# Causal mask of the key-major scores: added in the banks by VectorE instead of put there by TensorE

## The chip, the core and the metric

The kernel runs on one core of one Trainium2 chip. The metric is the device time of one execution in microseconds. Lower is better. Before the change the median of three runs is 4985.88 us (4983.53 to 4986.44).

## The reference

64 sequences of 256 tokens (x) with 256 channels go through two blocks. Each also has a context of 77 tokens. In short:

```
# block L0: cross attention to the context, 16 heads of 64
q0 = rms(x) @ wq ; k0, v0 = ctx @ wk, ctx @ wv
x  = x + softmax(q0 k0^T) v0 @ wo
# block L1, 16 heads of 16: causal self attention
z1 = ln(x)
q, k, v = z1 @ mq + b, z1 @ mk + b, z1 @ mv + b
scores  = q k^T / 4 ;  scores = where(t >= s, scores, -inf)
x  = x + softmax(scores) v @ m_proj + b
# then cross attention to the context, and the feed-forward layer
x  = x + attention(ln(x), ctx) @ c_proj + b
x  = x + relu(ln(x) @ f_w1 + b1) @ f_w2 + b2
```

All is float32. The kernel keeps that accuracy by splitting operands into a high and a low part and making three products for one.

## The kernel before

**Stages.** The keys and values of the context are made first for all sequences (steps ct, ka, va, up to about 330 us). Then every sequence ("batch" in the code) goes through the same steps, named in USES: turn.0 (transposes of x), q0, qs0.t.g (scores of block L0, queries on partitions), tr0 (transposes of the probabilities), pv0, wo; turn.1, q1.1, k1, v1, qsA and qsB (scores of the self attention, queries on partitions, used only for the maxima and sums of the rows), mt.1 (maxima plus logarithms of the sums, transposed, into maxT), skA.0, skA.1, skB (the same scores once more, but with keys on partitions: key-major), pv.1.0, pv.1.1, proj.1.0, proj.1.1; turn.2, q1.2, qs2, mt.2, sk2, pv.2, proj.2 (the second cross attention); turn.3, h.0 to h.3, f2.0, f2.1 (feed-forward, result to DRAM). rms, stat and norm are the statistics and the normalising, ln makes the logarithms' part of maxT's source. The last number is mostly a tile of 128 tokens or a half of the heads.

**Key-major scores.** skA.m has the first 128 keys against all 256 queries for the eight heads of half m. It fills four banks, one for each row r of the array of 32 partitions, with two heads to a bank. skB has the last 128 keys against the last 128 queries for all 16 heads, four heads to a bank. For each step TensorE makes, bank by bank, three kinds of products (lines 1566 to 1585): the mask on the diagonal blocks of 128 x 128 (line 1572: causal times a unit matrix, both bf16; it also starts the bank), minus the maxima and logarithms (line 1578, from maxT), the scores (line 1583, k1bd with q1T). ScalarE takes the exp of a whole bank of 512 (line 1041) into probs, and pv.1.m multiplies it with v1. The mask of the query-major scores (line 1531) is a product too, and is not touched.

**Order.** The loop is a software pipeline: in one turn TensorE does the steps of three sequences in the order written out in LOOP_ORDER_TEXT; a step with + belongs to the newest sequence, one with - to the oldest, and a step without a sign to the one between (the numbers after the colon are its banks). ScalarE and VectorE have their own written orders, ACT_ORDER_TEXT and DVE_ORDER_TEXT (after a slash: the part, one bank of four, or for qs0 the maximum 0 and the scaling 1). GpSimd and SyncE walk TensorE's order and do what belongs to them: GpSimd the inverse roots (line 904) and the additions of a bias row to xr and x1 (lines 919, 925), SyncE the loads and stores. There are 61 turns; HEAD and TAIL hold the steps ahead of the loop and behind it, with orders of their own. The last turns in the tail hold fewer sequences.

**Waits.** Every bank has two counting semaphores: full (TensorE is done with it) and free (its last reader is). take_bank waits for the bank's former reader, landed for the readers that made a step's operands. All engines run their orders strictly, so an instruction that waits holds up all that stand behind it on its engine. TensorE also passes 230 empty waits ahead of the work, which shift the place of its instructions.

## Time and profile before

| what | us |
|---|---|
| median of three runs | 4985.88 |
| the profiled execution, its own time | 4985.86 |
| its span in the profile | 4984.1 |
| TensorE busy | 4801.7 (96%) |
| ScalarE busy | 3932.9 (79%) |
| VectorE busy | 3063.4 (61%) |
| GpSimd busy | 538.1 (11%) |

The busy time of TensorE is a union of matmuls that overlap in the array, and their ends are modelled. So a step's cost on TensorE is better read from the start of its first matmul to the start of the next step's. A group's "idle before" is the time for which its engine stood still ahead of it, with what ended that. PEld is the loading of weights, which lies beside the matmuls.

### The profile page before, as it was taken

Reading aid. Unit: us, or ns where it says so; the run is one execution under the profiler, and the core shown is the slowest. Engines: PE = TensorE matmul, PEld = TensorE weight load, DVE = VectorE, ACT = ScalarE, POOL = GpSimd, SP = SyncE. Lnnn points to the kernel's source line nnn. Section 1 sums busy time; section 2 is a strip of 40 time slices with the busy share of each in tenths; the row PEclk is TensorE's granted clock in tenths of the full one; section 3 lists DMA queues with packets and bytes.
Section 4 is the critical chain, followed back from the end, with each engine's and each line's share of the span. In section 5 each row is a group of like instructions: output and inputs, shape, how many; then the busy total and the mean of one; then the engine's idle time right before and its main releaser. Section 6 shows DMA issues by size and latency. Waiting matters only on the chain.

```text
span 4984.1 us, 142324 instructions
## 1 busy us (share of the span) xinstructions
PE 4801.7 (96%) x47160; PEld 3896.2 (78%) x47160; DVE 3063.4 (61%) x8003; ACT 3932.9 (79%) x16437; POOL 538.1 (11%) x845
## 2 busy tenths in 40 slices
...
DMA packets 219919, 181.12 MB, mean 36 GB/s; under 512 B 111312, under 2 KB 203920, under 8 KB 219856
## 3 DMA queue, kind: packets, MB, share of 16 engines
...
q8 instruction: 38, 0.62, 0.1%
q14 instruction: 25, 0.20, 0.0%
...
## 4 chain that ended last, share of the span: by engine, by line
issue 61%; PE 26%; POOL 8%; DVE 3%; ACT 1%; POOLq 0%; DMA 0%; DVEq 0%; SPq 0%
PE ps L1398 7%; PE ps L1400 6%; PE ps L1399 6%; POOL xr L919 3%; POOL small L904 3%; PE ps L1594 3%; PE ps L1512 2%; POOL x L925 2%; DVE z L1183 1%; DVE stats L1161 1%; PE ps L1406 1%; DVE x L1298 1%; ACT ps L952 0%; PE ps L1611 0%; DVE mv L1165 0%
## 5 line engine op out<-in xcount | busy, mean ns | idle before, releaser
L952 ACT ACTIVATE ps<-ps,negmax 128x77 f32<-128x77 f32 (+2 forms) x6144 | 2082.7, 380 | 64.9 <-DVE negmax L1197 64.9
L952 ACT ACTIVATION_READ_ACCUMULATOR ps<-ps,negmax 128x1 f32 x6144 | 1526.4, 257 | 0.0
L1197 DVE TENSOR_REDUCE negmax<-ps 128x4 f32<-128x308 f32 (+2 forms) x1792 | 932.1, 561 | 575.6 <-PE ps L1502 380.2
L904 POOL TENSOR_TENSOR small<-small 128x1 f32<-128x1 f32 (+1 forms) x448 | 265.8, 593 | 3974.7 <-DVE small L1174 2137.1
L1041 ACT ACTIVATE probs<-ps 128x512 f32<-128x512 f32 x768 | 396.5, 604 | 321.0 <-PE ps L1583 321.0
L1502 PE MATMUL ps<-k0bd,q0T 128*128 128x154 f32 x2048 | 360.4, 298 | 0.1
L932 ACT COPY probs<-ps 77x512 f32<-77x512 f32 x512 | 286.8, 590 | 62.1 <-PE ps L1545 62.0
L1502 PEld LDWEIGHTS ps<-k0bd,q0T 128*128 128x128 f32 x2048 | 289.8, 191 | 27.0 <-issue 25.9
L1398 PE MATMUL ps<-hi_f,coTh 128*128 128x256 f32 x1024 | 303.4, 296 | 2.5 <-DVE coTl L1332 2.5
L1398 PE MATMUL ps<-zTh,hi_f 128*128 128x256 f32 x1024 | 300.8, 294 | 4.3 <-DVE zTl L1192 3.1
L1398 PE MATMUL ps<-xTh,hi_wq 128*128 128x256 f32 x1024 | 300.7, 294 | 4.3 <-issue 4.3
L1398 PE MATMUL ps<-hi_wo,coTh 128*128 128x256 f32 x1024 | 296.2, 289 | 2.1 <-ACT ps L952 2.1
L1545 PE MATMUL ps<-ident,rows 128*77 128x128 f32 x2048 | 292.1, 280 | 4.7 <-DVE rows L1274 0.4
L1399 PE MATMUL ps<-lo_f,coTh 128*128 128x256 f32 x1024 | 290.1, 283 | 0.0
L1400 PE MATMUL ps<-hi_f,coTl 128*128 128x256 f32 x1024 | 289.4, 283 | 0.0
L1399 PE MATMUL ps<-lo_wo,coTh 128*128 128x256 f32 x1024 | 289.4, 283 | 0.0
L1400 PE MATMUL ps<-hi_wo,coTl 128*128 128x256 f32 x1024 | 289.4, 283 | 0.0
L1400 PE MATMUL ps<-zTh,lo_f 128*128 128x256 f32 x1024 | 289.1, 282 | 0.0
L1399 PE MATMUL ps<-zTl,hi_f 128*128 128x256 f32 x1024 | 289.0, 282 | 0.0
L1399 PE MATMUL ps<-xTl,hi_wq 128*128 128x256 f32 x1024 | 287.7, 281 | 0.0
L1400 PE MATMUL ps<-xTh,lo_wq 128*128 128x256 f32 x1024 | 287.3, 281 | 0.0
L1545 PEld LDWEIGHTS ps<-ident,rows 128*77 128x77 f32 x2048 | 226.0, 147 | 75.9 <-issue 57.4
(226 smaller groups left out, 12477.7 us busy)
## 6 DMA issues: line engine op xcount, KB each, us to landing
keys_of<-kring SPq DMA_DIRECT2D x128, 154.0 KB, 1.9
k0bd<-keys_of SPq DMA_DIRECT2D x128, 154.0 KB, 3.2
...
```

Source lines behind the costliest of these rows:

```text
L904: nc.gpsimd.tensor_tensor(rstd[:, stage, ts], veps[:, stage, ts], minus_half[:, ts], ALU.pow).then_inc(rstd_ready[stage], 1)
L919: nc.gpsimd.tensor_tensor(xr[:, t, :], xs[:, t, :], row[:, k - 1, :], ALU.add).then_inc(xr_ready, 1)
L932: return nc.scalar.copy(o, i)
L952: ins = nc.scalar.activation(scores, scores, ACT.Exp, bias=negmax[w][:, t, h:h + 1], accum_out=sums[w][:, t, h:h + 1])
L1041: nc.scalar.activation(probs_slot(step, r), bank(s), ACT.Exp).then_inc(free[s], 1)
L1197: nc.vector.tensor_reduce(dst, bank(s)[:, 0:heads * width].rearrange("p (h k) -> p h k", h=heads), AX_X, ALU.max, negate=True).then_inc(ma ...
L1398: pe.matmul(o, lh, rh, start=first, stop=False)
L1399: pe.matmul(o, lh, rl, start=False, stop=False)
L1400: return pe.matmul(o, ll, rh, start=False, stop=last)
L1502: ins = pe.matmul(bank(s)[:, j * 2 * S:(j + 1) * 2 * S], q0T[:, m, t * P:(t + 1) * P], k0bd[:, m, :, :], start=True, stop=True)
L1545: ins = pe.transpose(bank(s)[0:S, j * P:(j + 1) * P], rows_of_four(t, g)[:, j * S:(j + 1) * S], ident[:])
L1594: ins = pe.matmul(bank(s)[D0 * e:D0 * e + D0, j * T:(j + 1) * T], v0[0:S, D0 * h:D0 * h + D0], probs_slot(("tr0", 0, i), e)[0:S, j * T:(j ...
```

## The change

The four mask products in front of skA.0, skA.1 and skB go. Their first product with maxT starts the bank now. VectorE gets a step for each bank: it waits for full, adds a mask tile causal_keys (bf16, made by GpSimd at the start) to the diagonal blocks in the bank, in place, and counts a new semaphore, masked, for which ScalarE's exp waits in place of full. An add has 2 x 128 elements in each partition for skA and 4 x 128 for skB. The mask for the query-major scores stays on TensorE. With this all orders, all banks of the steps, and the sequence to which tr0.0.0 and tr0.1.0 belong in a turn are written anew, in the loop, the end of the head and the tail. The tail's orders are now the loop's three times over with the missing steps left out.

```diff
-RINGS = {"bank": 8, "split": 1, "chain": 1, "max": 1, "summed": 1}
+RINGS = {"bank": 8, "split": 1, "chain": 1, "max": 1, "masked": 1, "summed": 1}
...
-    "skA": {"bank": 4}, "skB": {"bank": 4}, "sk2": {"bank": 4},
+    "skA": {"bank": 4, "masked": 4}, "skB": {"bank": 4, "masked": 4}, "sk2": {"bank": 4},
...
 LOOP_ORDER_TEXT = """
-rms+ pv.1.0:1 skA.1:4357 tr0.0.0-:6 qs0.0.2-:0 pv0.1-:4 pv.1.1:1 tr0.1.0-:3 qs0.1.2-:7 proj.1.0:1 norm.2.0
-proj.1.1:3 stat.2.0 pv0.0-:0 tr0.0.2-:4 tr0.0.3-:3 tr0.1.3-:1 tr0.1.2-:2 turn.0+:5 turn.2.0:7 turn.2.1:6 pv0.2-:2
-q1.2:4 pv0.3-:6 qs2.1:3541 q0.1+:2 qs2.0:0673 wo.0-:2 wo.1-:7 q0.0+:2 q0.3+:7 qs0.0.1+:6 turn.1.0-:1 mt.2:3
-turn.1.1-:0 sk2.0:3257 k1-:0 stat.2.1 q1.1-:3 sk2.1:5672 stat.1.0- ln.2 ln.1- pv.2.0:0 qs0.0.0+:3 qsB.1-:5614
-norm.0+ pv.2.1:7 v1-:2 proj.2.0:0 qsB.0-:6173 proj.2.1:0 stat.1.1- qs0.1.1+:5 norm.1.0- norm.1.1- q0.2+:2 qsA-:4106
-stat.3.0 norm.2.1 turn.3.0:5 turn.3.1:7 qs0.1.0+:3 tr0.0.1+:5 h.2:7 norm.3.0 h.0:5 stat.3.1 h.3:1 tr0.1.1+:6
-qs0.0.3+:4 h.1:7 norm.3.1 mt.1-:2 qs0.1.3+:0 skB-:2615 f2.0:7 skA.0-:1563 f2.1:7
+pv.1.0:4 rms+ stat.2.0 skA.1:0215 pv0.0-:6 qs0.0.2-:3 qs0.1.2-:4 pv.1.1:2 pv0.1-:7 proj.1.0:6 proj.1.1:0 tr0.1.2-:4
+tr0.0.2-:1 tr0.1.3-:3 pv0.2-:5 turn.2.0:3 turn.2.1:6 tr0.0.3-:1 turn.0+:2 q1.2:4 stat.2.1 pv0.3-:7 qs2.1:6243
+q0.1+:5 qs2.0:6017 ln.1- wo.0-:4 wo.1-:3 stat.1.0- qs0.0.1+:5 norm.2.0 q0.0+:4 q0.3+:0 mt.2:7 turn.1.0-:3
+turn.1.1-:6 norm.1.0- stat.1.1- sk2.0:1257 k1-:6 q1.1-:5 norm.2.1 sk2.1:7014 pv.2.0:3 qs0.0.0+:5 qsB.1-:1206
+pv.2.1:7 stat.3.0 v1-:4 ln.2 norm.3.0 proj.2.0:3 qsB.0-:7521 proj.2.1:0 qs0.1.1+:4 q0.2+:3 turn.3.0:6 qsA-:7051
+turn.3.1:6 tr0.0.1+:4 stat.3.1 qs0.1.0+:2 h.2:6 h.0:7 h.1:0 norm.3.1 h.3:6 tr0.0.0+:3 tr0.1.1+:5 qs0.0.3+:7
+norm.1.1- mt.1-:4 qs0.1.3+:3 skB-:1450 f2.0:6 skA.0-:4127 norm.0+ f2.1:5 tr0.1.0+:1
 """
 
 
 
 ACT_ORDER_TEXT = """
-pv.1.0 skA.1/0 skA.1/1 skA.1/2 skA.1/3 qs0.0.2 pv.1.1 pv0.1 tr0.1.0 tr0.0.0 qs0.1.2 tr0.0.2 pv0.0 tr0.1.3 tr0.1.2
-turn.2.0 turn.2.1 tr0.0.3 turn.0 pv0.2 q1.2 pv0.3 qs2.1/0 q0.1 qs2.1/3 qs2.0/2 qs2.0/1 qs2.1/2 qs2.0/0 qs2.0/3
-qs2.1/1 ln.2 q0.3 q0.0 mt.2 turn.1.0 turn.1.1 qs0.0.1 sk2.0/2 sk2.0/0 sk2.0/1 sk2.0/3 k1 q1.1 sk2.1/0 sk2.1/1 pv.2.0
-sk2.1/3 sk2.1/2 qs0.0.0 pv.2.1 qsB.1/2 qsB.1/1 qsB.1/0 v1 qsB.1/3 qsB.0/1 qsB.0/0 qs0.1.1 qsB.0/2 qsB.0/3 turn.3.0
-turn.3.1 qsA/1 tr0.0.1 qsA/3 qsA/0 qsA/2 ln.1 q0.2 tr0.1.1 mt.1 qs0.1.0 skB/1 skB/2 skB/3 qs0.0.3 skA.0/3 skA.0/2
-skB/0 skA.0/0 skA.0/1 qs0.1.3
+pv.1.0 skA.1/2 skA.1/3 skA.1/1 skA.1/0 pv0.0 qs0.0.2 pv.1.1 qs0.1.2 tr0.1.2 tr0.0.2 tr0.1.3 pv0.1 turn.2.0 turn.2.1
+pv0.2 tr0.0.3 turn.0 q1.2 pv0.3 qs2.1/0 qs2.1/2 qs2.1/3 q0.1 qs2.0/3 qs2.1/1 qs2.0/0 qs2.0/1 qs2.0/2 ln.2 qs0.0.1
+mt.2 turn.1.0 turn.1.1 q0.0 q0.3 sk2.0/0 sk2.0/2 sk2.0/3 sk2.0/1 k1 q1.1 sk2.1/1 sk2.1/2 sk2.1/0 pv.2.0 sk2.1/3
+qs0.0.0 pv.2.1 qsB.1/1 qsB.1/0 v1 qsB.1/2 qsB.1/3 qsB.0/0 qsB.0/1 qsB.0/3 turn.3.0 qs0.1.1 qsB.0/2 turn.3.1 q0.2
+qsA/0 qsA/1 qsA/2 qsA/3 ln.1 tr0.0.1 tr0.0.0 tr0.1.1 mt.1 qs0.1.0 qs0.0.3 skB/1 skB/0 skB/2 qs0.1.3 skA.0/0 skA.0/3
+skA.0/2 skA.0/1 skB/3 tr0.1.0
 """
 DVE_ORDER_TEXT = """
-pv.1.0 rms qs0.0.2/0 norm.0 qs0.0.2/1 pv.1.1 pv0.1 qs0.1.2/0 proj.1.0 stat.2.0 proj.1.1 qs0.1.2/1 stat.2.1 norm.2.0
-norm.2.1 turn.2.0 turn.2.1 turn.0 pv0.2 pv0.0 qs2.1/0 qs2.1/3 pv0.3 qs2.0/2 qs2.1/1 qs2.0/1 qs2.1/2 qs2.0/0 wo.0
-qs2.0/3 stat.1.0 norm.1.0 wo.1 stat.1.1 ln.2 norm.1.1 qs0.0.1/0 turn.1.0 turn.1.1 qs0.0.1/1 qs0.0.0/0 pv.2.0 qsB.1/1
-qsB.1/2 qsB.1/3 pv.2.1 qsB.1/0 qs0.0.0/1 proj.2.0 stat.3.0 qsB.0/1 qsB.0/0 qsB.0/3 qs0.1.1/0 proj.2.1 qsB.0/2
-stat.3.1 qs0.1.1/1 norm.3.0 norm.3.1 qsA/1 turn.3.0 turn.3.1 qs0.1.0/0 qsA/3 qsA/2 qsA/0 h.2/0 h.0/0 h.2/1 h.3/0
-ln.1 h.3/1 h.0/1 h.1/0 h.1/1 qs0.0.3/0 qs0.1.3/0 qs0.1.0/1 qs0.0.3/1 f2.0 f2.1 qs0.1.3/1
+rms skA.1/2 skA.1/3 skA.1/1 skA.1/0 pv.1.0 qs0.0.2/0 pv0.0 qs0.1.2/0 qs0.0.2/1 pv.1.1 norm.0 qs0.1.2/1 proj.1.0
+stat.2.0 proj.1.1 stat.2.1 norm.2.0 norm.2.1 turn.2.0 turn.2.1 pv0.2 pv0.1 turn.0 qs2.1/0 pv0.3 qs2.1/2 qs2.1/3
+qs2.0/3 qs2.0/0 qs2.1/1 qs2.0/1 qs2.0/2 wo.0 stat.1.0 norm.1.0 wo.1 qs0.0.1/0 stat.1.1 ln.2 norm.1.1 qs0.0.1/1
+turn.1.0 turn.1.1 qs0.0.0/0 pv.2.0 qsB.1/1 qsB.1/2 qsB.1/0 pv.2.1 qs0.0.0/1 qsB.1/3 proj.2.0 stat.3.0 qsB.0/0
+qsB.0/1 qsB.0/3 proj.2.1 norm.3.0 qs0.1.1/0 stat.3.1 qsB.0/2 turn.3.0 norm.3.1 qs0.1.1/1 qsA/0 turn.3.1 qsA/3 qsA/1
+qsA/2 qs0.1.0/0 h.2/0 h.2/1 h.0/0 h.1/0 h.0/1 ln.1 h.3/0 h.1/1 h.3/1 qs0.0.3/0 qs0.1.0/1 skB/1 skB/0 skB/2 qs0.0.3/1
+qs0.1.3/0 skB/3 skA.0/0 skA.0/3 skA.0/1 skA.0/2 f2.0 qs0.1.3/1 f2.1
...
+        elif "masked" in uses:
+            given["masked"].append((key, part, 0))
...
+        causal_keys = sb("causal_keys", [P, P], BF16)
...
-        maxed = sem("maxed")
+        maxed, masked = sem("maxed"), sem("masked")
...
+            nc.gpsimd.affine_select(out=causal_keys[:], in_=causal_keys[:], compare_op=ALU.is_ge, fill=MASKED, base=0,
+                                    pattern=[[1, P]], channel_multiplier=-1).then_inc(consts_made, 1)
...
                     elif n in ("skA", "skB"):
-                        s = landed(u, r)
+                        (s, _, _), (_, _, n_masked) = u["bank"][r], u["masked"][r]
+                        act.wait_ge(masked, n_masked)
                         nc.scalar.activation(probs_slot(step, r), bank(s), ACT.Exp).then_inc(free[s], 1)
...
+                    elif n in ("skA", "skB"):
+                        s, v, _ = u["bank"][r]
+                        heads = 2 if n == "skA" else 4
+                        diagonal = bank(s).rearrange("p (h q) -> p h q", h=heads)[:, :, 0:P]
+                        dve.wait_ge(full[s], v)
+                        nc.vector.tensor_tensor(diagonal, diagonal, causal_keys[:].unsqueeze(1).to_broadcast([P, heads, P]),
+                                                ALU.add).then_inc(masked, 1)
...
-            for _ in range(230):
+            for _ in range(226):
...
-                        for r in range(4):
-                            s = take_bank(u, r)
-                            diagonal = bank(s).rearrange("p (h q) -> p h q", q=cols)[:, :, 0:P]
-                            pe.matmul(diagonal, causal[:], identb[:].unsqueeze(1).to_broadcast([P, len(heads), P]),
-                                      start=True, stop=False, skip_group_check=True)
                         for j, (m, e) in enumerate(heads):
                             for r in range(4):
-                                s, rs = u["bank"][r][0], slice(32 * r, 32 * r + 32)
+                                s, rs = take_bank(u, r) if j == 0 else u["bank"][r][0], slice(32 * r, 32 * r + 32)
                                 h = 8 * m + 2 * r + e
                                 pe.matmul(bank(s)[:, j * cols:(j + 1) * cols], head_of32[rs, h:h + 1].to_broadcast([32, P]),
-                                          maxT[0][rs, qs], start=False, stop=False, skip_group_check=True)
+                                          maxT[0][rs, qs], start=(j == 0), stop=False, skip_group_check=True)
                         for j, (m, e) in enumerate(heads):
```


The orders of head and tail are not shown. In both the masks stand on VectorE as in the loop; the head's new orders differ from sequence 0's turn.0 on.

## Rows read from the trace of the kernel before

**Rows 1.** The page's head and its busy time by engine.
```profile
span 4984.1 us, 142324 instructions
...
PE 4801.7 (96%) x47160; PEld 3896.2 (78%) x47160; DVE 3063.4 (61%) x8003; ACT 3932.9 (79%) x16437; POOL 538.1 (11%) x845
```

**Rows 2.** Windows of loop and end: length, busy by engine, granted clock, DMA.
```profile
480.00:4800.00 4320.00, 4222.33 (x42740) 3398.49 (x42740) 2766.18 (x7310) 3619.02 (x15285) 505.83 (x788) 1.00 0.09 24
4800.00:4984.10 184.10, 139.43 (x1360) 110.26 (x1358) 85.90 (x220) 105.53 (x434) 16.13 (x25) 0.89 0.04 10
```

**Rows 3.** Waits from 480 to 4800 us: waiter, releaser, total, times, longest.
```profile
ACT probs L1041 <- PE ps L1583: 305.4, 181, 2.1
...
PE ps L1406 <- DVE z L1183: 67.7, 121, 1.2
```

**Rows 4.** Chain of waits in order of time: start, length, what.
```profile
2564.22 0.42 DVE z L1183
...
2635.72 0.42 DVE z L1183
```

**Rows 5.** Timeline of TensorE, 2540 to 2557 us: start, length, line, tile, count.
```profile
2540.30 1.02 PE L1572 MATMUL ps<-identb,causal 128*128 128x512 bf16 x4
2541.25 0.67 PE L1578 MATMUL ps<-maxT,head_of 32*128 32x128 f32 x16
...
2547.60 0.39 PE L1398 MATMUL ps<-hi_f,coTh 128*128 128x256 f32 x1
...
2550.67 1.07 PE L1611 MATMUL ps<-probs,v 128*32 128x256 f32 x16
...
2552.11 0.61 PE L1572 MATMUL ps<-identb,causal 128*128 128x256 bf16 x4
2552.65 0.51 PE L1578 MATMUL ps<-maxT,head_of 32*128 32x256 f32 x8
...
2553.95 0.66 PE L1545 MATMUL ps<-ident,rows 128*77 128x128 f32 x4
...
2555.07 1.08 PE L1594 MATMUL ps<-probs,v 77*64 77x256 f32 x8
2556.17 1.07 PE L1611 MATMUL ps<-probs,v 128*32 128x256 f32 x16
```

**Rows 6.** Groups by line and shape, whole span: busy us, mean ns of one.
```profile
L1192 DVE TENSOR_TENSOR coTl<-ps,coTh 128x512 fp32r<-128x512 f32 x256 | 169.6, 684 | 6.8 <-ACT coTh L932 3.0
...
L1311 DVE TENSOR_TENSOR xs<-ps,x 128x256 f32<-128x256 f32 x128 | 54.3, 425 | 9.2 <-PE ps L1400 1.2
...
L952 ACT ACTIVATION_READ_ACCUMULATOR ps<-ps,negmax 128x1 f32 x6144 | 1526.4, 257 | 0.0
...
L952 ACT ACTIVATE ps<-ps,negmax 128x256 f32<-128x256 f32 x1024 | 469.4, 473 | 4.4 <-DVE negmax L1197 4.4
```

**Rows 7.** Timeline of ScalarE at skA.1.
```profile
2554.05 2.07 ACT L1041 ACTIVATE probs<-ps 128x512 f32<-128x512 f32 x4 [1.43 <-PE ps L1583]
```

**Rows 8.** Timelines of VectorE, GpSimd and TensorE up to turn.2.1.
```profile
2559.79 0.42 DVE L1311 TENSOR_TENSOR xs<-ps,x 128x256 f32<-128x256 f32 x1
...
2561.24 0.42 DVE L1311 TENSOR_TENSOR xs<-ps,x 128x256 f32<-128x256 f32 x1
...
2561.28 0.73 POOL L919 TENSOR_TENSOR xr<-xs,row 128x256 f32<-128x256 f32 x1 [5.97 <-DVE small L1174]
...
2564.69 0.44 PE L1406 MATMUL ps<-ident,z 128*128 128x128 f32 x2 [0.42 <-DVE z L1183]
```

**Rows 9.** Timeline of TensorE at turn.3.0 and at sk2.0 of two turns.
```profile
2530.85 0.76 PE L1406 MATMUL ps<-ident,z 128*128 128x128 f32 x4 [0.68 <-DVE z L1183]
...
2582.72 0.67 PE L1555 MATMUL ps<-maxT,head_of 32*77 32x256 f32 x8 [0.29 <-ACT maxT L932]
```

**Rows 10.** Timeline of VectorE over the loop's edge.
```profile
2551.85 0.48 DVE L1274 TENSOR_TENSOR rows<-ps,over 128x308 f32<-128x308 f32 x1
...
2552.65 0.42 DVE L1192 TENSOR_TENSOR aTl<-ps,aTh 128x256 fp32r<-128x256 f32 x1 [0.32 <-ACT aTh L932]
```

More of the change, by code:

```diff
@@ L171 @@
+wo.0@0 qs0.1.1@1/0 qs0.0.0@1/0 stat.1.0@0 wo.1@0 stat.1.1@0 norm.1.0@0 norm.1.1@0 qs0.0.1@1/0 turn.1.0@0 turn.1.1@0
+qs0.0.0@1/1 qs0.0.1@1/1 qs0.1.1@1/1 qs0.1.0@1/0 w.12@0 qsA@0/1 qs0.1.0@1/1 qsA@0/3 qsA@0/0 qsA@0/2 qsB.1@0/1
+qsB.1@0/3 qsB.1@0/0 qsB.1@0/2 qsB.0@0/2 qsB.0@0/0 qsB.0@0/3 qsB.0@0/1 qs0.1.3@1/0 ln.1@0 skB@0/1 skB@0/2 skB@0/3
+skB@0/0 skA.0@0/0 skA.0@0/2 skA.0@0/1 skA.0@0/3 qs0.0.3@1/0 qs0.1.3@1/1 qs0.0.3@1/1
 """
 TAIL_ORDER_TEXT = """
-tr0.0.0@1:4 pv.1.0@0:2 ln.2@0 rms@2 skA.1@0:6735 norm.2.0@0 pv0.1@1:2 stat.2.0@0 stat.2.1@0 tr0.1.0@1:0 qs0.1.2@1:4
```

151 lines of the change are left out of this document (75 added, 76 removed).

## Prediction

> **What bounds the kernel now.** I read the page's busy table first, then the windows, then the waits, then single turns. TensorE is busy 4801.7 us of a span of 4984.1 us, ScalarE 3932.9, VectorE 3063.4 [rows 1]. By stretch, the loop's body (480 to 4800 us) has TensorE busy 4222.33 of 4320 us at a granted clock of 1.00, so it has under 98 us of gaps in some 60 turns, 1.6 us in each; the tail (4800 on) has a clock of 0.89 and more gaps [rows 2]. The waits say what the gaps are: TensorE waits for VectorE's z before the transposes, 67.7 us [rows 3]; the 305.4 us that ScalarE waits for the key-major scores cost nothing, since the reader has to see that ScalarE is the faster engine there. The period is read from the chain of work: the same z starts at 2564.22 and at 2635.72, so a turn takes 71.50 us [rows 4], and 61 turns are 4361.5 us. A microsecond off TensorE's order in a turn is worth 61 in the kernel, as long as no new wait takes its place. That is the whole question.
>
> **Mask products removed from TensorE.** In a turn 12 products go: four of 512 columns (skB) and eight of 256 (two skA). Start to start, skB's four take 2540.30 to 2541.25, 0.95 us, and each skA's four take 2552.11 to 2552.65, 0.54 us [rows 5]. Together 2.03 us a turn. What follows them has the same change of operand shape before it as they had, so I count no more.
>
> **Adds put on VectorE.** A turn gets eight adds over 256 elements and four over 512. No row shows VectorE writing a bank, nor a bf16 operand of this shape. The nearest rows are its adds and subtractions that read a bank: 0.42 us for 256 elements, 0.684 for 512 [rows 6]. From below, a gain through the 2-byte operand is excluded as long as the other operand is 4-byte in a bank, so 0.42 and 0.68 stand as the lower end; from above the nearest row that reads a bank and writes it in place is ScalarE's exp of 256 elements, 0.473 us, with its accumulator read 0.257 in all 0.73 [rows 6], and by the same ratio 1.19 for 512. I take 0.42 and 0.68 because these rows share engine, operation and source: 8 x 0.42 + 4 x 0.68 = 6.1 us a turn; the far end is rival D. VectorE was busy 2766.18 us in the 4320 of the loop [rows 2], 46 us a turn; it goes to 52 of about 70. It does not become the bound on average. What counts is who waits for an add.
>
> **Wait in front of pv.1.1 (skA.1, adds, exp, pv.1.1).** Before: the scores end at 2553.95, ScalarE's four exps run from 2554.05 for 2.07 us [rows 7], and pv.1.1 starts at 2556.17, behind 2.22 us of other steps: tr0 and qs0 1.12, pv0 1.10 [rows 5]. Step lengths here and below are such distances from start to start; a qs0 is 0.6, a product of the three-product groups 0.12. So there was nearly no wait. After: first add 0.05 + 0.42, hand-over 0.1, then ScalarE at its own pace (2.07, since an add is shorter than an exp): 2.65 us. Cover: pv0.0 1.10 and two qs0, 2.32 us (2 x 0.62 less a little overlap). New wait 0.33 us. Queued behind the adds on VectorE are pv.1.0's low part and pv0.0's; on ScalarE, behind the exps, pv0.0's copy and qs0.0.2's exps.
>
> **Wait in front of pv.1.0.** skA.0 ends, then f2.1 (24 products; 2.9 us of the 3.07 from 2547.60 to 2550.67 [rows 5]) and tr0.1.0 (0.5) cover 3.4 us; the adds, four exps and skB/3's exp, put last by the order, need about 3.15. No wait, 0.25 us to spare.
>
> **Stretch to turn.2.1.** This is where I think the new order is worse. VectorE's order from pv.1.1's end is: pv.1.1's low part (not before 1.0, since ScalarE does qs0.0.2's exps, 1.3 us, first), norm.0 0.6, qs0.1.2/1 0.65, then xs, statistics, xs, statistics at 1.45 each (2559.79 to 2561.24 [rows 8]), then z and z. TensorE is asked for pv0.1 1.05, two proj 1.45, three tr0 1.4, pv0.2 1.05. By hand: proj.1.0 waits until 1.45 (0.4), turn.2.0's z ends at 5.85 against TensorE there at 5.4 (0.45), turn.2.1's at 6.7 (0.5). The rows of before show one wait there, 0.42 [rows 8]. The order also has a gain in it: GpSimd now does the root of stat.2.0 before the 0.7 us addition to xr, which stood in front of it (2561.28 [rows 8]); without it the waits were longer still. In this half-turn, from pv.1.0 to the end of wo.1, waits grow by 0.33 + 0.4 + 0.45 + 0.5 - 0.42 = 1.26, and by 0.1 for bank 4, which wo.0 gets from the second third of qs2.1's exps: +1.36 us.
>
> **Stretch from wo.1 to pv.1.0.** mt.2 now stands before both turn.1 steps, so maxT is copied while they run: the wait of 0.29 [rows 9] and the shortened start beside it go, -0.4. turn.3.0 moves ahead of qsA, which fills the time of the second z: the wait of 0.68 [rows 9] goes; in its place qsA waits 0.35 for bank 1 (the third part of qsB.0 on ScalarE), and tr0.0.1 0.25 for bank 4; other orders (proj.2.1 no longer late, qsB's banks) give 0.1. Late next is skB, 0.3 us for bank 0 behind h.1's low part on VectorE; the same density (VectorE had little rest at 2600 to 2608) was paid before as well, in the trace hidden in busy TensorE, so I count it 0. Sum -0.58.
>
> **Moves that weigh nothing.** The tr0.0.0 and tr0.1.0 steps move over the loop's edge: one copy fewer in the tail, one more in the head. DMAs: k0's and v0's loads are issued where their last reader stands, within a few us of before, and no TensorE row waits for one; kc's and vc's readers keep their places; out goes behind f2.1 as before. SP is past nothing new. On GpSimd one memset and one select, some 0.5 us at the start, lie beside the load of the first windows, which TensorE waits for. Four waits fewer in TensorE's padding before the loop are nanoseconds.
>
> **Sum.** A turn: -2.03 + 1.36 - 0.58 = -1.25, so 70.25 us; 61 turns -76. Head: 1.5 us of masks and the same waits, -2. Tail (219 us from 4764): three batches' masks are 4.6 us less, but its order is now the loop's order with the missing steps left out, with holes where they were, and at the very end TensorE waits for each result, so an add replaces a product there at no gain: -1, between -5 and +6. Span 4984.1 - 79 = 4905. The profiled execution was 4985.86 us, 1.8 over its span and equal to the median of 4985.88, so 4907.
>
> **The clock.** The granted clock in the loop is 1.00, the 2.4 GHz level, with gaps of up to 0.68 us in it [rows 2, 9]; the new gaps are of that size, so I leave it there. The Trainium skill (VectorE: DVE Perf Modes, Rules for kernel authors) advises to minimise the number of VectorE operations, as every one ends with a drain of its own; by that alone this change is the wrong way round. The trace allows it, for VectorE has room on average [rows 2].
>
> **Rivals.**
> A, the sum above: 4907, own range 4885 to 4935. Chance 0.52.
> B, the waits do not grow: my hand-made 1.36 is wrong, as ScalarE does qs0.0.2 earlier or norm.0 is cheaper. For: the largest terms hang on 0.1 us steps. Against: rows 8 show this chain late already. 64 x 2.03 = 130: 4856. Chance 0.20.
> C, the waits eat it all: late adds hold banks (skB's four adds stand between h.3's low parts and f2.0 in VectorE's fullest stretch, and skA.0's exps come after qs0.1.3's, which wait for its maximum behind three adds). Another 0.5 to 1.25 us a turn: 4938 to 4985. Chance 0.18, of it 0.09 still faster, 0.06 no change, 0.03 slower.
> D, slower: the add itself is dear. For: no row shows a write into a bank by VectorE. Once an add over 256 elements takes d > 0.5, the adds set the pace of the exps: pv.1.1 waits 0.05 + 4d + 0.1 + 0.5 - 2.32 = 4d - 1.67, which is 4d - 2.0 more than in the sum, and pv.1.0 waits 0.5 more behind 3.4 us of cover, 4d - 2.25. Together 8d - 4.25, so the 1.25 is gone at d = 0.69. At the upper bound of 0.73 it is 1.59 - 1.25 = +0.34 us a turn, 21 in the loop: 5007. Against: that bound is far, and belongs to another engine [rows 6]. Chance 0.06.
> E, slower: the loop's backward branch. TensorE passed it under f2.1's 2.9 us of queued products; now only tr0.1.0's 0.5 stands there. For it, if the branch costs up to the whole old cover, is 2.4 us a turn: 5051. Against: VectorE passes the same edge between 2552.33 and 2552.65 [rows 10], under 0.32 us. Chance 0.04. The Trainium skill (Runtime: NRT & Kernel Launch, Instruction fetch mechanics) says that a taken branch out of the fetched window stalls until its page is there; by that rule this rival would be real, and the trace at this edge does not bear it out.
> That the products stay is excluded: they are deleted.
>
> **Range and chances.** Low end 4850 takes in B, high end 4965 most of C; D, E and the rest of C are left out. Faster by over 0.2% (10 us, about what a measurement tells): 0.52 + 0.20 + 0.09 = 0.81; within it 0.06; slower 0.13.
>
> **What would show it.** No 128x256 or 128x512 bf16 product in front of maxT's; the period of z at 70.25; VectorE adds near 0.42 and 0.68; ScalarE's wait at probs now ended by VectorE; TensorE waiting some 0.3 at pv.1.1 and 0.4 to 0.5 at both turn.2 steps, and not for maxT. A period under 69.7 means B, one over 71 means C, adds over 0.69 mean D, a gap between tr0.1.0 and pv.1.0 means E.

## The result

The changed kernel takes 4955.0 us (median of 4, 4951.0 to 4956.8) against 4984.7 us (4982.3 to 4986.4) for the kernel before: a ratio of 0.9939, 95% interval 0.9923 to 0.9955. It is 30 us faster, 0.6%, clear of the interval; 79 were forecast. 4955 lies inside the stated range of 4850 to 4965. Its profiled execution took 4954.4 us with a span of 4952.5.

The page's head and busy times after the change [answers to rows 1]: TensorE 74 us less, VectorE 342 us more.
```profile
span 4952.5 us, 142533 instructions
...
PE 4727.5 (95%) x46392; PEld 3870.7 (78%) x46392; DVE 3405.4 (69%) x8771; ACT 3941.1 (80%) x16437; POOL 540.4 (11%) x847
```

The window of the loop [rows 2] (length, busy by engine in the order PE, PEld, DVE, ACT, POOL, then granted clock, DMA share, GB/s). In it TensorE now has 134.5 us of gaps, 97.7 before. (From 480 to 4700 us, which in both kernels is loop alone, they are 131.9 and 94.6.)
```profile
480.00:4800.00 4320.00, 4185.48 (x42474) 3400.72 (x42476) 3120.05 (x8114) 3663.11 (x15434) 510.99 (x793) 1.00 0.09 24
```

TensorE's waits from 480 to 4800 us [rows 3] (waiter, releaser, total, times, longest): nearly all are waits that come once in each of the 61 turns, 0.17 to 0.41 us long.
```profile
PE ps L1422 <- DVE z L1192: 25.2, 61, 0.4
PE ps L1605 <- ACT probs L940: 22.8, 61, 0.4
PE ps L1414 <- DVE aTl L1201: 19.3, 61, 0.3
...
PE ps L1589 <- DVE coTl L1348: 11.0, 61, 0.2
PE ps L1518 <- DVE aTl L1201: 10.6, 61, 0.2
...
```

The adds themselves [rows 6] (busy, mean ns of one, idle before): 0.425 and 0.690 us, where 0.42 and 0.68 were taken.
```profile
L1299 DVE TENSOR_TENSOR ps<-ps,causal_keys 128x256 f32<-128x256 f32 x512 | 182.5, 425 | 111.2 <-PE ps L1594 111.2
L1299 DVE TENSOR_TENSOR ps<-ps,causal_keys 128x512 f32<-128x512 f32 x256 | 164.6, 690 | 5.6 <-PE ps L1594 5.6
```

GpSimd's one instruction of this shape in a turn gives the period [rows 4]: 70.83 us, where 70.25 was forecast and 71.50 was before.
```profile
2535.98 0.71 POOL L912 TENSOR_TENSOR small<-small 128x2 f32<-128x2 f32 x1 [21.45 <-DVE small L1180]
...
2606.81 0.71 POOL L912 TENSOR_TENSOR small<-small 128x2 f32<-128x2 f32 x1 [21.45 <-DVE small L1180]
```

From the start of the first pv.1.0 of the loop to that of the first behind it, and to the end, the two traces divide so (us):

| part | before | after | difference | forecast |
|---|---|---|---|---|
| head, to 402.84 / 407.63 | 402.8 | 407.6 | +4.8 | -2 |
| loop, 61 turns, to 4768.16 / 4728.64 | 4365.3 | 4321.0 | -44.3 | -76 |
| tail, to the end of the span | 215.9 | 223.9 | +8.0 | -1 |

One turn of TensorE in the changed kernel [rows 5, 8]. A number in brackets at the end of a row is the time for which TensorE stood still ahead of it, and what ended that. The first row is pv.1.0; 2607.22 is the end of skA.1's scores, 2609.99 pv.1.1, 2612.83 proj.1.0, 2618.17 turn.2.1, 2626.20 wo.0, 2632.06 the step behind wo.1.
```profile
2604.48 1.07 PE L1622 MATMUL ps<-probs,v 128*32 128x256 f32 x16
...
2607.22 1.08 PE L1605 MATMUL ps<-probs,v 77*64 77x256 f32 x8
...
2609.20 0.79 PE L1518 MATMUL ps<-k0bd,q0T 128*128 128x154 f32 x4 [0.17 <-DVE aTl L1201]
2609.99 1.07 PE L1622 MATMUL ps<-probs,v 128*32 128x256 f32 x16
...
2612.83 0.38 PE L1414 MATMUL ps<-hi_mp,aTh 128*128 128x256 f32 x1 [0.32 <-DVE aTl L1201]
...
2616.20 1.08 PE L1605 MATMUL ps<-probs,v 77*64 77x256 f32 x8 [0.37 <-ACT probs L940]
...
2618.17 0.44 PE L1422 MATMUL ps<-ident,z 128*128 128x128 f32 x2 [0.41 <-DVE z L1192]
...
2626.20 0.39 PE L1414 MATMUL ps<-hi_wo,coTh 128*128 128x256 f32 x1 [0.24 <-ACT ps L960]
...
2632.06 0.69 PE L1518 MATMUL ps<-k0bd,q0T 128*128 128x154 f32 x4
```

From pv.1.0 to wo.1's end (the start of the step behind it) is 27.58 us (27.37 before, 2550.67 to 2578.04); the rest of the turn is 43.25 us (44.13 before). These are called the first and second half turn below. The end of the turn, where skB (2665.38), f2.0 (2667.43), f2.1 (2671.79) and tr0.1.0 (2674.78) stand ahead of the next pv.1.0:
```profile
2665.38 0.33 PE L1589 MATMUL ps<-maxT,head_of 32*128 32x128 f32 x3
2665.90 0.66 PE L1589 MATMUL ps<-maxT,head_of 32*128 32x128 f32 x13 [0.20 <-DVE coTl L1348]
...
2667.43 0.39 PE L1414 MATMUL ps<-hi_f,coTh 128*128 128x256 f32 x1
...
2674.78 0.60 PE L1561 MATMUL ps<-ident,rows 128*77 128x128 f32 x4
2675.31 1.07 PE L1622 MATMUL ps<-probs,v 128*32 128x256 f32 x16
```

### The profile page after: what moved, and what is told of

The parts are those of the page before. It is cut to its first block, busy times and chain, and to the rows that moved or that the text cites. A ratio compares the mean times of both kernels' runs of the same rounds, so it can differ in the third digit from the quotient of the medians.

```text
span 4952.5 us, 142533 instructions
## 1 busy us (share of the span) xinstructions
PE 4727.5 (95%) x46392; PEld 3870.7 (78%) x46392; DVE 3405.4 (69%) x8771; ACT 3941.1 (80%) x16437; POOL 540.4 (11%) x847
## 4 chain that ended last, share of the span: by engine, by line
issue 78%; PE 9%; POOL 9%; ACT 2%; DVE 1%; POOLq 0%; DMA 0%; SPq 0%; DVEq 0%
POOL small L912 4%; POOL xr L927 3%; PE ps L1414 3%; PE ps L1416 2%; PE ps L1415 2%; POOL x L933 2%; ACT ps L960 1%; POOLq L911 0%; PE ps L1622 0%; PE ps L1576 0%; PE ps L1481 0%; DVE negmax L1206 0%; DMA keys_of<-kring 0%; PE ps L1594 0%; ACT probs L1050 0%
## 5 line engine op out<-in xcount | busy, mean ns | idle before, releaser
L960 ACT ACTIVATION_READ_ACCUMULATOR ps<-ps,negmax 128x1 f32 x6144 | 1587.8, 268 | 0.0
L1206 DVE TENSOR_REDUCE negmax<-ps 128x4 f32<-128x308 f32 (+2 forms) x1792 | 943.3, 562 | 637.5 <-PE ps L1518 410.7
L1050 ACT ACTIVATE probs<-ps 128x512 f32<-128x512 f32 x768 | 410.7, 600 | 140.1 <-DVE ps L1299 140.1
L1299 DVE TENSOR_TENSOR ps<-ps,causal_keys 128x256 f32<-128x256 f32 (+1 forms) x768 | 347.1, 513 | 116.8 <-PE ps L1594 116.8
L1518 PE MATMUL ps<-k0bd,q0T 128*128 128x154 f32 x2048 | 372.7, 304 | 11.4 <-DVE aTl L1201 11.0
L1518 PEld LDWEIGHTS ps<-k0bd,q0T 128*128 128x128 f32 x2048 | 289.8, 191 | 76.1 <-issue 50.6
L1605 PE MATMUL ps<-probs,v 77*64 77x256 f32 x2048 | 277.2, 391 | 23.7 <-ACT probs L940 23.7
```

What stands on the lines that cost most here:

```text
L960: ins = nc.scalar.activation(scores, scores, ACT.Exp, bias=negmax[w][:, t, h:h + 1], accum_out=sums[w][:, t, h:h + 1])
L1050: nc.scalar.activation(probs_slot(step, r), bank(s), ACT.Exp).then_inc(free[s], 1)
L1206: nc.vector.tensor_reduce(dst, bank(s)[:, 0:heads * width].rearrange("p (h k) -> p h k", h=heads), AX_X, ALU.max, negate=True).then_inc(ma ...
L1299: nc.vector.tensor_tensor(diagonal, diagonal, causal_keys[:].unsqueeze(1).to_broadcast([P, heads, P]), ALU.add).then_inc(masked, 1)
L1518: ins = pe.matmul(bank(s)[:, j * 2 * S:(j + 1) * 2 * S], q0T[:, m, t * P:(t + 1) * P], k0bd[:, m, :, :], start=True, stop=True)
L1605: ins = pe.matmul(bank(s)[D0 * e:D0 * e + D0, j * T:(j + 1) * T], v0[0:S, D0 * h:D0 * h + D0], probs_slot(("tr0", 0, i), e)[0:S, j * T:(j ...
```

## Experiments

Ratios are to the kernel before, run on the same chip, with 95% intervals.

**One half of the change at a time.** New orders, banks and batch places with the mask still on TensorE:
```
-    VectorE: tensor_tensor(diagonal, diagonal, causal_keys, ADD)      (12 a turn)
+    TensorE: matmul(bank, identb, causal, start=True)                 (12 a turn, as before)
```


> The orders, banks and batch places of the changed kernel, but the mask is again added by TensorE's products (no adds on VectorE). Theory O: the new orders are worth no more than the old ones: period 70.83 + 2.03 less the 0.4 us wait of pv.1.1 = 72.2 to 72.6 us, 5035 to 5065 us, slower than the kernel before. Theory V: without the adds the waits of the first half turn (proj.1.0, pv0.2, turn.2.1, wo.0, some 1.4 us) go as well: period 71.0 to 71.5 us, 4960 to 4990 us, no slower than before.

Measured: 5011.2 us, ratio 1.0051 (1.0037 to 1.0065). The orders alone make the kernel slower. A turn of its TensorE (first pv.1.0, the mask products of skA.1, the scores' end, pv.1.1, then the waits):
```profile
2562.06 1.07 PE L1608 MATMUL ps<-probs,v 128*32 128x256 f32 x16
...
2563.50 0.61 PE L1569 MATMUL ps<-identb,causal 128*128 128x256 bf16 x4
...
2565.34 1.08 PE L1591 MATMUL ps<-probs,v 77*64 77x256 f32 x8
...
2567.65 1.07 PE L1608 MATMUL ps<-probs,v 128*32 128x256 f32 x16
...
2570.48 0.38 PE L1395 MATMUL ps<-hi_mp,aTh 128*128 128x256 f32 x1 [0.31 <-DVE aTl L1189]
...
2575.82 0.44 PE L1403 MATMUL ps<-ident,z 128*128 128x128 f32 x2 [0.41 <-DVE z L1180]
```
Its end, mask products of skB at 2622.98, f2.0 at 2625.49, mask products of skA.0 at 2628.46, f2.1 at 2630.30, next pv.1.0 at 2633.80:
```profile
2622.98 1.04 PE L1569 MATMUL ps<-identb,causal 128*128 128x512 bf16 x4
...
2625.49 0.38 PE L1395 MATMUL ps<-hi_f,coTh 128*128 128x256 f32 x1
...
2633.80 1.07 PE L1608 MATMUL ps<-probs,v 128*32 128x256 f32 x16
```
Its period, from pv.1.0 to pv.1.0, is 71.74 us. Taken in this sequence, the change divides into orders, +0.24 (71.50 to 71.74), and mask, -0.91 (71.74 to 70.83); the next experiment shows that in the old orders the mask's share is another one, so these are not two effects that simply add. The mask's products were 2.05 us, so 1.14 came back, and the two traces say where.

At skA.1: from the scores' end to pv.1.1 are 2.31 us with products, 2.77 with adds (+0.46). ScalarE's exps end 0.05 to 0.06 us ahead of pv.1.1 in both, and with the adds they start 0.46 us later behind the scores (0.65 us in place of 0.19); with products first, then with adds:
```profile
2565.53 2.06 ACT L1038 ACTIVATE probs<-ps 128x512 f32<-128x512 f32 x4 [1.52 <-PE ps L1580]
```
```profile
2607.87 2.07 ACT L1050 ACTIVATE probs<-ps 128x512 f32<-128x512 f32 x4 [1.44 <-DVE ps L1299]
```
0.54 us of products went there, and from pv.1.0 to wo.1's end the turns take 27.60 and 27.58 us. **The eight products of the two skA are not alike: skA.1's four were worth nothing.**

At skB: from skB to f2.0 are 2.51 us with products, 2.05 with adds, where 0.97 us of products went (+0.51). From f2.0 to skA.0 are 2.97 and 3.06 us (+0.09). VectorE is not later there with the adds: the low parts of h.1 (the first two of these four instructions, which free bank 0) and of h.3 start at 2622.57 with products and at 2664.98 with adds, 0.41 and 0.40 us ahead of skB's first product (2622.98, 2665.38). With products first, then with adds:
```profile
2622.57 1.65 DVE L1329 SCALAR_TENSOR_TENSOR coTl<-ps,minus_bias,coTh 128x256 fp32r<-128x256 f32 x4
```
```profile
2664.98 1.65 DVE L1348 SCALAR_TENSOR_TENSOR coTl<-ps,minus_bias,coTh 128x256 fp32r<-128x256 f32 x4
```
Bank 0 comes free at the same place in both. A mask product of skB takes 0.24 us of the 0.97, and the one for bank 0 is the fourth, so with products this bank was asked for some 0.7 us behind skB's start; without them it is asked for almost at once.

The time lies between the two theories' ranges, but the traces decide for O: the waits of 0.31, 0.37 and 0.41 us in the first half turn are the same without a single add, so they belong to the order. From 480 to 4800 us the list of TensorE's waits is that of the changed kernel without two rows: skB's (L1589, 11.0 us) and the one for bank 4 ahead of qs0.1.2 (L1518, 10.6 us). The second is behind VectorE's adds, and this one is V's share; the first comes from the products' leaving.

The other half, the adds in the old orders and banks, each group put on VectorE ahead of the exps that need it:
```
-LOOP_ORDER, ACT_ORDER, DVE_ORDER, heads, tails: new        +the ones of the kernel before
+DVE_ORDER: ... skB/1 skB/2 skB/3 skB/0 qs0.0.3/1 skA.0/3 skA.0/2 skA.0/0 skA.0/1 f2.0 f2.1 ...
```


> VectorE adds the mask, as in the changed kernel, but every order, bank and batch place is the one of the kernel before (the adds are put into VectorE's old order in front of the exps that need them). Theory O (the new orders give back what the masks bring): the 2.03 us of products go, pv.1.1 waits about 0.45 us longer for its first exp since the old cover of 2.22 us was just enough, and nothing else grows much: period 71.50 - 2.03 + 0.45 = 69.9 to 70.4 us, head and tail as before: 4895 to 4925 us, faster than the changed kernel. Theory V (VectorE is the loss: 6 us more a turn make its chains late wherever they stand): the z, low-part and statistics steps of the old order come later, period 70.8 or more, 4950 or more.

Measured: 5275.4 us, ratio 1.058 (1.0566 to 1.0595). Theory O was far too low, and theory V, whose "4950 or more" holds it, gave no size. VectorE, then TensorE, in one turn: f2.1 needs the bank of f2.0, f2.0's addition (L1358) stands behind skA.0's adds, and f2.1 waits 2.23 us. The last fence is the window of f2.1 (granted clock ahead of the last two numbers).
```profile
2684.89 1.42 DVE L1299 TENSOR_TENSOR ps<-ps,causal_keys 128x256 f32<-128x256 f32 x4
2686.21 0.41 DVE L1358 TENSOR_TENSOR xr<-ps,xr 128x256 f32<-128x256 f32 x1
```
```profile
2686.74 0.58 PE L1414 MATMUL ps<-hi_f,coTh 128*128 128x256 f32 x1 [2.23 <-DVEq L1361]
```
```profile
2686.74:2692.16 5.42, 5.42 (x25) 5.20 (x25) 0.00 (x0) 2.38 (x11) 0.00 (x0) 0.50 0.00 0
```
f2.1 then ran at 0.50, the 1.2 GHz level, and took 5.4 us; at 2.4 GHz the same 24 products take 2.99 us in the changed kernel (2671.79 to 2674.78). So in this turn the wait cost 2.2 us and the clock 2.4 more.

One word moved (and the same word at one place in the tail):
```
-... qs0.0.3/1 skA.0/3 skA.0/2 skA.0/0 skA.0/1 f2.0 f2.1
+... qs0.0.3/1 f2.0 skA.0/3 skA.0/2 skA.0/0 skA.0/1 f2.1
```


> The first experiment (adds in the orders and banks of the kernel before) with one word moved in VectorE's order, in the loop and in the tail: f2.0's addition, which frees the bank that f2.1 needs, now stands ahead of skA.0's four adds and not behind them. Theory P (what an add costs is what is queued behind it on VectorE; a gap of 2.23 us there also drops TensorE's granted clock for the next 2.9 us of products): the 2.23 us wait and the slow f2.1 (5.4 in place of 2.9 us) go, a turn takes 70.0 to 71.5 us in place of 76, 4915 to 4985 us. Rival (the adds make VectorE late all over the old order): no less than 73.5 us a turn, 5100 us or more.

Measured: 5107.6 us, ratio 1.0242 (1.0226 to 1.0258), period 73.26 us. The word is worth 168 us, wait and clock together, so theory P has the mechanism: what stands behind the adds is what they cost. Its size was wrong; the time is in the rival's range (5100 or more) and the period just under its 73.5, since other steps stand behind adds in the old order as well:
```profile
2616.48 0.36 PE L1414 MATMUL ps<-hi_mp,aTh 128*128 128x256 f32 x1 [0.65 <-DVE aTl L1201]
...
2677.86 0.39 PE L1414 MATMUL ps<-hi_f,coTh 128*128 128x256 f32 x1 [0.89 <-DVEq L1361]
```
The adds need orders made for them. I placed them, so this says nothing on the best old-style order.

**How the time goes with an add's length.**
```
-diagonal = bank(s)[:, :, 0:P];  in1 = causal_keys                 (skA: 2 x 128 columns)
+diagonal = bank(s)[:, :, 0:2P]; in1 = causal_keys, second half 0  (skA: 2 x 256 columns)
```


> The changed kernel with skA's eight adds a turn made over 512 elements in place of 256 (the second half of the mask is zeros, so the values are the same); measured rows give 0.61 us start to start in place of 0.33. Theory T (the adds stand in the path of pv.1.1, which comes 2.77 us behind the scores' end, 2.31 without adds): four adds set the pace of ScalarE's exps, pv.1.1 comes 0.4 to 0.5 us later, and at skA.0 0 to 0.4 us more: 0.4 to 0.9 us a turn, 4980 to 5010 us. Rival (VectorE has room, only the hand-over to ScalarE counts): within 5 us of the changed kernel's 4955.

Measured: 5073.0 us, ratio 1.0178 (1.0164 to 1.0192), period 72.55: 1.72 us a turn more, about twice theory T's upper end; the rival is out. Most of it stands at two places. VectorE and TensorE at skA.1 (scores' end 2593.12, pv.1.1 2596.89):
```profile
2593.29 2.49 DVE L1299 TENSOR_TENSOR ps<-ps,causal_keys 128x512 f32<-128x512 f32 x4 [0.96 <-PE ps L1594]
2595.70 0.41 DVE L1200 TENSOR_TENSOR aTl<-ps,aTh 128x256 fp32r<-128x256 f32 x1
```
```profile
2596.16 0.79 PE L1518 MATMUL ps<-k0bd,q0T 128*128 128x154 f32 x4 [1.24 <-DVE aTl L1200]
2596.89 1.07 PE L1622 MATMUL ps<-probs,v 128*32 128x256 f32 x16
```
pv.1.1 comes 3.77 us behind the scores, 1.00 later than in the changed kernel, and not for its exps: pv.1.0's low part stands behind all four adds and holds bank 4, which qs0.1.2 needs. In the changed kernel the same wait is there, 0.17 us long (row 2609.20). The second place is tr0.1.0 at the end of the turn, which now waits 0.6 us for a bank that ScalarE's exps of skA.0 still hold:
```profile
2662.32 0.66 PE L1561 MATMUL ps<-ident,rows 128*77 128x128 f32 x4 [0.62 <-ACT probs L1049]
```
So the cover of 3.4 us there, 0.25 to spare by the prediction, is used up once the adds are twice as long.

**Head and tail.** The tail, then the head, in the old order with adds put in:
```
-TAIL_ORDER, TAIL_ACT_ORDER, TAIL_DVE_ORDER: new       +the ones of the kernel before, adds put in
```


> The changed kernel with the tail (all that follows the loop) in the order and banks of the kernel before, VectorE's adds put in. Theory O: the tail of the changed kernel is the loop's order with the missing steps left out, and its holes cost the 8 us by which it is longer: tail 213 to 217 us in place of 223.9, 4944 to 4949 us. Rival: the tail is long because results arrive one after the other and TensorE's clock falls in it whatever the order: 4953 to 4960 us.


```
-HEAD_ORDER, HEAD_ACT_ORDER, HEAD_DVE_ORDER: new
+the ones of the kernel before, adds put in, tr0.0.0@1:7 tr0.1.0@1:6 behind tr0.1.1@1
```


> The changed kernel with the head (all that stands before the loop) in the order and banks of the kernel before, adds put in; tr0.0.0 and tr0.1.0 of the next batch are put behind the old order's last transposes. Theory O: the 4.8 us by which the loop starts later come from the new head order, whose waits are longer and keep TensorE at the low clock for 14 us: the loop starts at 401 to 404 us in place of 407.6, 4948 to 4951 us. Rival: the head's loss comes with the adds, in front of the exps of skB and skA.0: it stays, 4953 to 4957 us.

Measured: 4952.0 us (0.9932, 0.9918 to 0.9945) and 4950.5 us (0.9925, 0.9911 to 0.9939), neither told apart from the changed kernel's 0.9939 by intervals. The traces say more. The tail, from its first pv.1.0: 215.9 us before, 220.0 with new orders and products, 223.9 with new orders and adds, 220.9 with the old order and adds, more than theory O's 213 to 217. Over all traces of this study it takes 221.9 to 224.2 us with new orders and adds (six traces) and 218.3 to 220.9 with the old order and adds (three), so differences under some 2.5 us say nothing. In the tail order and adds so cost some 4 us each, though 28 mask products, 5.1 us of TensorE's busy time in the run with products, left with the latter.

The loop's first pv.1.0: 402.84 before, 407.41 with new orders and products, 407.63 with new orders and adds, 406.31 with the old head and adds. Ten traces with the new head have it at 405.3 to 408.2, so 406.31 is not told apart from them, and it is above theory O's 401 to 404: Theory O falls for the head. The 1.5 us of products bring nothing there. Some 1.0 us of the 4.8 is the work of the two tr0 steps, which moved into the head and for which the sum had nothing. The rest is gaps: from 340 us to the first pv.1.0 TensorE is busy 53.58 us of 62.84 before and 53.76 of 67.63 after, at granted clocks of 0.88 and 0.87. The windows of the three tails (before, products in new orders, changed) say where the time stands:
```profile
4768.16:4984.10 215.94, 169.80 (x1675) 135.56 (x1674) 105.61 (x275) 129.94 (x543) 21.11 (x33) 0.91 0.05 14
```
```profile
4786.09:5006.10 220.01, 173.64 (x1671) 136.15 (x1670) 106.25 (x273) 129.09 (x538) 21.16 (x33) 0.88 0.05 14
```
```profile
4728.64:4952.50 223.86, 177.04 (x1643) 140.10 (x1642) 117.52 (x301) 130.01 (x538) 21.08 (x33) 0.83 0.05 14
```
TensorE's gaps hardly differ (46.1, 46.4, 46.8 us). It is busy 7.2 us longer with fewer instructions, at a granted clock of 0.83 in place of 0.91, so by this account the new tail's loss stands in the lower clock. Most of that is one stretch: from 4881 to 4934 us of the changed kernel the granted clock is 0.51, with TensorE busy 28.4 us of 53, and all six traces with this tail have a stretch of the same length and clock. It depends on the order: with the old tail and adds TensorE is busy 171.4 us at 0.87 and has 49.5 us of gaps, so there more of the loss is gaps. How long the new tail would be at the clock of before, no run shows.

**Taking waits out of the changed kernel.** First, the wait at skB for bank 0:
```
-DVE_ORDER: ... h.0/1 ln.1 h.3/0 h.1/1 h.3/1
+DVE_ORDER: ... h.0/1 ln.1 h.1/1 h.3/0 h.3/1
```


> The changed kernel with h.1's low part ahead of h.3's high part in VectorE's loop order: bank 0, for which skB's fourth quarter waits, comes free at about 2665.0 in place of 2665.85. Theory S (of the 0.97 us that skB's products took, half is given back as a wait for this bank, behind VectorE's fullest stretch): the 0.2 us wait and the 0.3 us of slow start around it go, 0.2 to 0.45 us a turn, 4927 to 4943 us. Rival (it returns in front of f2.0, whose last operand is the low part of h.3, or at pv.1.0): 4950 to 4957 us.

Measured: 4930.9 us, ratio 0.9887 (0.9871 to 0.9902), period 70.44: theory S. skB has no wait (2654.51 to f2.0 at 2656.12 is 1.61 us, 2.05 in the changed kernel), nothing is late in its place. One word is worth 24 us, nearly as much as the whole change.
```profile
2654.51 0.74 PE L1589 MATMUL ps<-maxT,head_of 32*128 32x128 f32 x16
...
2656.12 0.39 PE L1414 MATMUL ps<-hi_f,coTh 128*128 128x256 f32 x1
```

Second, the waits of the first half turn, in the changed kernel's loop:
```
-LOOP_ORDER: tr0.1.3:3 pv0.2:5 turn.2.0:3 turn.2.1:6 tr0.0.3:1 turn.0:2
+LOOP_ORDER: tr0.1.3:3 tr0.0.3:2 pv0.2:5 turn.2.0:3 turn.2.1:6 turn.0:1   (ScalarE alike)
-DVE_ORDER: pv.1.1 norm.0 qs0.1.2/1 ... norm.2.0 norm.2.1
+DVE_ORDER: pv.1.1 qs0.1.2/1 ... norm.2.0 norm.0 norm.2.1
```


> The changed kernel with the loop's order changed between proj.1.1 and turn.0: tr0.0.3 stands ahead of pv0.2 (fills the wait of 0.37 us for probs), and on VectorE norm.0 stands behind norm.2.0, so that both z of the half turn come earlier. Theory O (the 1.3 us of waits between pv.1.1 and wo.0 are a matter of order, since they are the same, 0.31, 0.37, 0.41, 0.15 and 0.24 us, with the mask on TensorE): 0.4 to 0.8 us a turn less, 4905 to 4932 us. Rival (they are pushed on to the next reader: the exps of qs2.1, whose pace ScalarE sets): under 0.15 us a turn, 4946 us or more.

Measured: 4961.2 us, ratio 0.9947 (0.9933 to 0.996), period 70.88: the rival in substance, at another place than it said. pv0.2's wait is gone, and behind the transposes 0.57 and 0.56 us stand in for 0.41:
```profile
2621.82 0.44 PE L1422 MATMUL ps<-ident,z 128*128 128x128 f32 x2 [0.57 <-DVE z L1192]
...
2623.25 0.38 PE L1414 MATMUL ps<-zTh,hi_cq 128*128 128x256 f32 x1 [0.56 <-DVE zTl L1201]
```

Then with the bank 0 word kept, norm.0 in a gap of VectorE (without, and with, tr0.0.3 ahead of pv0.2), and the old tail:
```
-DVE_ORDER: qs0.0.2/0 pv0.0 ... pv.1.1 norm.0 qs0.1.2/1
+DVE_ORDER: qs0.0.2/0 norm.0 pv0.0 ... pv.1.1 qs0.1.2/1
```


> The last experiment (h.1's low part ahead of h.3's high part) and one word more: norm.0 stands on VectorE behind the maxima of qs0.0.2, in a stretch of 0.9 us in which VectorE waits for ScalarE's coTh, and no longer ahead of the statistics of proj.1.0. Theory Z (in the first half turn the chain proj.1.0, statistics, z, transpose sets the pace, and norm.0's 0.6 us stand in it): both z come 0.4 to 0.65 us earlier, the wait of 0.41 us in front of turn.2.1 goes: 0.3 to 0.5 us a turn under 70.44, 4900 to 4913 us. Rival (pv0.2's wait for its copy and the exps of qs2.1 on ScalarE hold the pace): within 5 us of 4931.

> As the kernel with both words moved, and tr0.0.3 ahead of pv0.2 on TensorE and ScalarE. That step alone moved the loss from pv0.2 to the z and to the low part of z (waits of 0.57 and 0.56 us). Theory Z: with z 0.6 us earlier the first of the two goes, the second stays: the same as without the step, within 8 us of it. Rival (the step fills a wait, and a filled wait is gained): 15 to 25 us less than without it.

> As the kernel with both words moved, with the tail in the order and banks of the kernel before. With the loop of the changed kernel that tail was 3 us shorter in the trace and 3 us in the medians: 3 us under the kernel with both words moved alone; rival: no difference, since the tail is bound by results that arrive one after the other.

Measured: 4932.5 us (0.9893, 0.9876 to 0.9909), 4933.2 us (0.9893) and 4928.9 us (0.9886, 0.9869 to 0.9902). Against the kernel with the bank 0 word alone (4930.9) neither of the first two brings anything; the filled wait of the second is not gained, so its rival falls. In the first theory Z falls: norm.0's 0.6 us turn into idle time of VectorE, which waits for ScalarE's exps of qs0.1.2 and comes to proj.1.0's statistics no sooner. The third is 3.6 us under the first, as expected, but within the intervals; their tails take 220.6 and 221.9 us.
```profile
2603.35 0.18 DVE L1282 RECIPROCAL over<-sums 128x4 f32<-128x4 f32 x1 [0.51 <-ACT ps L960]
```

Last, on top of the third:
```
-DVE_ORDER: qs0.1.2/0 qs0.0.2/1 pv.1.1
+DVE_ORDER: qs0.1.2/0 pv.1.1 qs0.0.2/1
```


> As the last experiment (both words moved, old tail), and on VectorE pv.1.1's low part ahead of the normalisation of qs0.0.2, behind which it stood 0.3 us longer than ScalarE's high part was there. Theory Q (the chain that paces the first half turn begins at proj.1.0, which waits 0.32 us for exactly this low part): proj.1.0, the transposes behind it and the wait for their copy come 0.3 us earlier: 0.2 to 0.3 us a turn, 4911 to 4918 us. Rival (the next reader is late instead: the exps of qs0.1.2 on ScalarE set when VectorE gets to the statistics, and the z come no earlier): under 0.1 us a turn, 4923 us or more.

Measured: 4922.0 us (4921.7 to 4922.7), ratio 0.9875 (0.9859 to 0.9892), the fastest kernel of the study, 33 us under the changed one. Its period is 0.09 us shorter than without the word (70.36 against 70.45): the rival. That is 5 to 6 us, and the intervals of the two kernels overlap. proj.1.0 waits no more, 0.31 us earlier in the turn, and the z before turn.2.0 takes 0.19 of it back:
```profile
2599.20 0.38 PE L1413 MATMUL ps<-hi_mp,aTh 128*128 128x256 f32 x1
...
2603.87 0.44 PE L1421 MATMUL ps<-ident,z 128*128 128x128 f32 x2 [0.19 <-DVE z L1191]
```

## Why the prediction was right in direction and wrong in size

The run with the new orders and the products on TensorE lets the sum be compared with what was measured, part by part (us a turn, differences; the two transposes that moved, 1.0 us, are in the orders):

| part | orders, forecast | orders, measured | mask moved, forecast | mask moved, measured |
|---|---|---|---|---|
| first half turn | +0.03 | +0.23 | -0.21 | -0.02 |
| second half turn | +0.42 | +0.01 | -1.49 | -0.89 |
| turn | +0.45 | +0.24 | -1.70 | -0.91 |

The loop missed by 0.58 us a turn: 0.79 too much expected of the mask, less 0.21 by which the orders were better than forecast.

- **Mask products, -2.03 us a turn:** 2.05 (0.54 + 0.97 + 0.54). Right.
- **Adds 0.42 and 0.68 us:** 0.425 and 0.690. Right; rival D (0.69 for the short one) is out.
- **Wait in front of pv.1.1, 2.65 us behind the scores against a cover of 2.32:** 2.77 against 2.31. The hand-over from the scores to the first add took 0.1 us more, and so skA.1's 0.54 us of products came back by 0.46 here. The mechanism, exps that start later behind the adds, was right. The low part of pv.1.0 behind the adds, which I named and did not price, is a second path that ends at the same time here; the wide adds made it the longer one.
- **No wait in front of pv.1.0:** right, and rival E is out, since pv.1.0 follows tr0.1.0 with no wait (2674.78, 2675.31), with only those 0.5 us queued over the branch. By the Trainium skill (Runtime: NRT & Kernel Launch, Instruction fetch mechanics) a stall could stand here; in this trace none reaches TensorE.
- **proj.1.0 +0.4, both z +0.45 and +0.5:** proj.1.0 waits 0.32, turn.2.1 0.41, and the third wait stands one step earlier, at pv0.2 (0.37). turn.2.1 comes 6.75 us behind pv.1.1's end, 6.7 was forecast. The kernel with products shows the same waits: a matter of the order, as the prediction had it.
- **The rest of the first half:** pv.1.0 to wo.1's end was to take 27.19 us (27.37, less 0.54 of products and 1.0 of two transposes that left, and 1.36 of waits) and took 27.58. The 0.39 are 0.12 at pv.1.1 and some 0.3 between turn.2.1 and wo.0: more than the 0.1 given for bank 4, as qs2.0 and wo.0 both stand behind ScalarE's exps of qs2.1.
- **"Late next is skB, 0.3 us for bank 0 behind h.1's low part ... so I count it 0":** this is the step that failed. The premise was that the wait had been paid before as well, hidden in busy TensorE. That held only because the products stood over it, and they were being removed. With them skB runs unhindered (2622.98), without them it stops for bank 0, which VectorE frees at the same place in both, and 0.51 of their 0.97 us come back. Taking the wait away gave 24 us. With the 0.46 at pv.1.1, of which I had 0.33, and 0.09 at skA.0, moving the mask brings 0.91 us a turn where the working had 1.70 (2.03 less 0.33).
- **Second half turn:** 43.06 us by the sum (44.13 + 1.0 of transposes moved in, - 1.49 of products, - 0.58), 43.25 measured. That it is so near is luck, two errors that nearly cancel: the orders brought 0.99 us there (45.13 to 44.14 with products) where I had 0.58, and 0.60 at skB and skA.0 was missing. Which of the moves brought the 0.41 more, no run separates.
- **Head -2, tail -1 (up to +6):** +4.8 and +8.0. Here the sum failed a second time. In the tail it went as its warning said, and further: an add replaced a product at no gain, and the granted clock of the whole tail fell from 0.91 to 0.83, with TensorE busy 7.2 us longer. I had left the clock alone on the strength of the loop's rows. What the head's new order costs was not forecast at all, and which of its waits carries it stays open; so does what in the tail's order lowers its clock. The loop is 32 of the 48 us that were missed, head and tail are the rest.

Loop -76 became -44, head and tail -3 became +13: together the 48 us by which the forecast missed. Rival B is out, since the waits did grow. 4955 lies outside the own range of the forecast (4885 to 4935) and in that of rival C (4938 to 4985), and a part of C's mechanism is there: the stretch around skB, where it put the loss, has 0.51 us of it. But it is not the adds that hold a bank at skB; bank 0 is held by h.1's low part, ahead of them in VectorE's order, and for as long with the products on TensorE.
